# Reading final LSTM states for their transposes straight from the batch-innermost tile, with the score stage unrolled

## The reference, cut to what matters

```python
h = jnp.maximum(_layernorm(x, axis=-1), 0.0)
x = x + _L2_gnn_ref(h, ...)      # LSTMs over windows of 1 to 4 nodes: the final states
h = jnp.maximum(_layernorm(x, axis=-1), 0.0)
x = x + _L3_gnn_ref(h, ...)      # attention over 256 edges
...
# in _L3_gnn_ref
Xq = (H @ W_lin.T).reshape(bt, n, h, dh)
Xv = (H @ W_val.T).reshape(bt, n, h, dh)
Qs = Xq[:, src]
Kt = Xq[:, dst]
e = jnp.einsum('behd,hd->beh', jax.nn.leaky_relu(Qs + Kt, LRELU_SLOPE), a)
```

## Time and profile before

| | us |
|---|---|
| median of 3 runs | 1331.84 (1330.07 to 1332.06) |
| the profiled execution, its own time | 1332.54 |
| its span in the trace | 1330.8 |
| PE busy | 1204.2 (90%) |
| DVE busy | 1047.3 (79%) |
| ACT busy | 944.5 (71%) |
| POOL busy | 381.8 (29%) |
| first instruction of the score stage on ACT, from the span's start | 1015.86 |
| last `q_sums` of the score stage begins | 1174.54 |

### The profile page before, as it was taken

One profiled execution on the slowest core, in us unless ns is written; L12 is line 12 of the kernel. 1 busy time (PEld: TensorE's weight loads), 2 busy tenths in 40 slices (PEclk: granted clock), 3 DMA queues, 4 the chain that ended last, 5 costly groups with the idle time before them and its releaser, 6 DMA issues. The chain is left out here.

```text
span 1330.8 us, 23570 instructions
## 1 busy us (share of the span) xinstructions
PE 1204.2 (90%) x6704; PEld 967.9 (73%) x6704; DVE 1047.3 (79%) x2081; ACT 944.5 (71%) x1745; POOL 381.8 (29%) x770
## 2 busy tenths in 40 slices
PE   3999979979889998999999999999996999936998
PEld 2999876643368886798789878978984777724777
DVE  4777857987778876988798779878874899986775
ACT  2666648857668876877787778767766999814775
POOL 2566750000067420000000000000001566615885
PEclk8999998989979999999999999999997999977999
DMA  7000000000031110000000000003003000000212
GB/s 295 1 0 0 0 0 0 0 0 0 30 113 63 71 41 1 0 1 0 1 0 1 0 1 1 1 0 127 1 0 127 1 1 0 1 0 8 79 71 95
DMA packets 14461, 37.80 MB, mean 28 GB/s; under 512 B 1856, under 2 KB 3904, under 8 KB 13120
## 3 DMA queue, kind: packets, MB, share of 16 engines
q1 hardware_dynamic: 13008, 36.31, 7.1%
q10 hardware_dynamic: 1392, 0.74, 0.2%
HBM read 20.27 MB, written 16.78 MB: 28 GB/s over the span
## 5 line engine op out<-in xcount | busy, mean ns | idle before, releaser
L955 ACT ACTIVATE gates<-bank,lstm_bias 128x512 f32<-128x512 f32 (+1 forms) x504 | 301.8, 637 | 101.8 <-PE bank L944 88.8
L139 ACT ACTIVATE l_h<-X,nmr,rstd 128x128 f32 (+1 forms) x512 | 210.2, 485 | 54.3 <-POOLq L133 32.9
L108 POOL TENSOR_TENSOR l2r_sum<-l2r_st 128x8 f32<-128x8 f32 x16 | 3.4, 210 | 532.8 <-DVE l2r_st L89 532.5
L929 PE MATMUL bank<-lstm_node_hi,Wih_hi 128*128 128x512 f32 (+1 forms) x408 | 149.0, 365 | 0.0
L930 PE MATMUL bank<-lstm_node_hi,Wih_lo 128*128 128x512 f32 (+1 forms) x408 | 148.8, 365 | 0.0
L931 PE MATMUL bank<-lstm_node_lo,Wih_hi 128*128 128x512 f32 (+1 forms) x408 | 148.7, 365 | 0.0
L940 PE MATMUL bank<-lstm_hid_hi,Whh_hi 128*128 128x512 f32 (+1 forms) x288 | 104.2, 362 | 4.7 <-DVE lstm_hid_hi L1011 4.5
L944 PE MATMUL bank<-lstm_hid_lo,Whh_hi 128*128 128x512 f32 (+1 forms) x288 | 106.7, 370 | 0.0
L941 PE MATMUL bank<-lstm_hid_hi,Whh_lo 128*128 128x512 f32 (+1 forms) x288 | 103.3, 359 | 0.0
L960 ACT ACTIVATE gates<-lstm_cell 128x512 f32<-128x512 f32 (+1 forms) x144 | 83.7, 581 | 21.7 <-DVE lstm_cell L998 21.5
L929 PEld LDWEIGHTS bank<-lstm_node_hi,Wih_hi 128*128 128x128 f32 x408 | 76.9, 189 | 11.6 <-ACT gates L955 0.3
(11 more groups left out here) (252 smaller groups left out, 3304.6 us busy)
## 6 DMA issues: line engine op xcount, KB each, us to landing
X<-in_x SPq DMA_DIRECT2D x8, 1024.0 KB, 14.1
x_spill<-X SPq DMA_DIRECT2D x32, 256.0 KB, 2.0
X<-x_spill SPq DMA_DIRECT2D x2, 4096.0 KB, 12.6
out<-X SPq DMA_DIRECT2D x32, 256.0 KB, 2.0
w_raw<-in_WihT SPq DMA_DIRECT2D x1, 1024.0 KB, 5.3
w_raw<-in_WhhT SPq DMA_DIRECT2D x1, 1024.0 KB, 7.5
W<-in_L_W ACTq DMA_DIRECT2D x1, 192.0 KB, 4.8
rows<-in_rows ACTq DMA_DIRECT2D x1, 128.0 KB, 4.3
```

What stands on the lines that cost most here:

```text
L139: last = act.activation(h[:, j, :], k.X[:, bass.ds(b0, TB), :][:, j, :], ACT.Relu, bias=k.nmr[:, bass.ds(b0, TB)][:, j:j + 1], scale=k.rst ...
L929: pe.matmul(out, hi, x_high, start=True, stop=False)
L955: act.activation(gate_of(it, g), k.bank[4 * s + g][:, 0:it.N], ACT.Tanh if g == GATE_G else ACT.Sigmoid, bias=k.lstm_bias[:, it.p - 1, g:g ...
```

## The change

The stage is written out turn by turn with constant addresses (no hardware loops, no register arithmetic, no semaphores counted up by one ahead). `Residual` is no longer used there. ACT's fetch and the two buffers `l2r_o` are gone; PE's transposes take each batch of a tile straight out of `HT`, so the stationary operand is 128 floats a partition with a step of 64 bytes. The waits for the fetch are gone on PE. The order of everything else on each engine is as before, and so is the DMA.

```diff
 def stage_scores(k, ctx, HT, Xv, scores, e):
...
-    res = Residual(k, ctx, "l2r", S, {}, psR)
+    ln = LayerNormTail(k, ctx, "l2r", S)
     tail_in = sem("l3_x_tail")
-    HALF = n_it // 4 - AHEAD // 2
...
+    states = HT[:, :].rearrange("h (g n b) -> h g n b", n=P, b=GROUP)
+    rows = lambda i, s: slice((i * S + s) * TB, (i * S + s + 1) * TB)
+    TAIL = k.B // 2 // (TB * S)
...
         def _(act):
-            def fetched(place, ahead):
-                return in_group(HT, place, ahead).rearrange("h n b -> h b n")
...
+            for i in range(n_it):
                 for s in range(S):
                     act.wait_ge(R["Tp"][s], i + 1)
                     act.activation(hT[s][:, :, :], as_tile(psT[s]), ACT.Copy).then_inc(R["hT"][s], 1)
-                if place:
-                    for s in range(S):
-                        act.wait_ge(res.R_ready[s], i + AHEAD + 1)
-                        res.fetch(act, s, fetched(place, (AHEAD + 1) * S + s))
...
         def _(pe):
+            def turn_over(i, s):
+                if i:
+                    pe.wait_ge(R["updated"][s], i)
+                for j in range(TB):
+                    b = (i * S + s) * TB + j
+                    last = pe.transpose(psR[s][:, j * P:(j + 1) * P], states[:, b // GROUP, :, b % GROUP], k.ident[:, :])
+                last.then_inc(R["R"][s], 1)
+
+            for i in range(AHEAD):
+                for s in range(S):
+                    turn_over(i, s)
+            for i in range(n_it):
                 for s in range(S):
                     pe.wait_ge(R["h"][s], i + 1)
                     for j in range(TB):
                         last = pe.transpose(psT[s][:, j * P:(j + 1) * P], h[s][:, j, :], k.ident[:, :])
                     last.then_inc(R["Tp"][s], 1)
-                    if residual:
-                        pe.wait_ge(res.updated[s], i + AHEAD)
-                        res.turn_over(pe, i + AHEAD, s)
+                    if i + AHEAD < n_it:
+                        turn_over(i + AHEAD, s)
```

More of the change, by code:

```diff
@@ L1189, in _ @@
         def _(pool):
-            def turn(i, place, residual, following):
+            ln.open(pool)
+            for i in range(AHEAD):
+                ln.coefficients(pool, i)
+            for i in range(n_it):
                 for s in range(S):
-                    pool.wait_ge(R["lin"][s], i + 1)
+                    if i:
+                        pool.wait_ge(R["lin"][s], i)
                     pool.wait_ge(R["Xq"][s], i + 1)
@@ L1196, in turn @@
                                        op=ALU.mult).then_inc(R["Qs"][s], 1)
-                if residual:
-                    res.coefficients(pool, i + AHEAD)
-            res.ln.open(pool)
-            for s in range(S):
[L1202 to L1205, removed]
+                if i + AHEAD < n_it:
+                    ln.coefficients(pool, i + AHEAD)
         @block.scalar
         def _(act):
-            def fetched(place, ahead):
-                return in_group(HT, place, ahead).rearrange("h n b -> h b n")
             def normalise(i, s):
-                res.ln.wait(act, s, i)
+                ln.wait(act, s, i)
                 normalise_tile(act, k, h[s], (i * S + s) * TB).then_inc(R["h"][s], 1)
-            def turn(i, place, residual, following):
+            for s in range(S):
+                normalise(0, s)
+            for i in range(n_it):
                 for s in range(S):
@@ L1228, in turn @@
                     act.wait_ge(R["V"][s], i + 1)
-                    act.activation(Xv[:, bass.ds((i * S + s) * TB, TB), :], as_tile(psV[s]), ACT.Copy).then_inc(R["Xv"][s], 1)
-                    if following:
+                    act.activation(Xv[:, rows(i, s), :], as_tile(psV[s]), ACT.Copy).then_inc(R["Xv"][s], 1)
+                    if i + 1 < n_it:
                         normalise(i + 1, s)
[L1233 to L1240, removed]
         @block.tensor
         def _(pe):
-            def turn(i, place, residual, following):
+            def turn_over(i, s):
+                if i:
+                    pe.wait_ge(R["updated"][s], i)
[3 more added lines that the diff above has]
+                last.then_inc(R["R"][s], 1)
+            for i in range(AHEAD):
+                for s in range(S):
+                    turn_over(i, s)
+            for i in range(n_it):
                 for s in range(S):
@@ L1264, in turn, with _, update @@
                         pe.matmul(ps[:, :], e.PT[:, c * P:(c + 1) * P], Xq[s][:, :, :], start=True, stop=True).then_inc(R["G"][s], 1)
-            for s in range(S):
-                pe.sem_inc(R["M"][s], 1)
+        @block.vector
+        def _(dve):
+            def update(i):
+                if i == TAIL:
+                    dve.wait_ge(tail_in, 16)
+                for s in range(S):
+                    xt = X[:, rows(i, s), :]
+                    dve.wait_ge(R["R"][s], i + 1)
+                    dve.tensor_tensor(xt, as_tile(psR[s]), xt, ALU.add).then_inc(R["updated"][s], 1)
+                for s in range(S):
+                    dve.wait_ge(R["updated"][s], i + 1)
+                    ln.stats(dve, X[:, rows(i, s), :], s, i)
             for i in range(AHEAD):
+                update(i)
+            for i in range(n_it):
+                if i + AHEAD < n_it:
+                    update(i + AHEAD)
                 for s in range(S):
                     if i:
[L1271 to L1281, removed]
+                        dve.wait_ge(R["kept"][s], i)
                     for c, ps in enumerate((psQ[s], psV[s])):
@@ L1288, in turn @@
                 for s in range(S):
[L1289 to L1292, removed]
+                    t = i * S + s
+                    dve.wait_ge(R["M"][s], i + 1)
+                    dve.tensor_reduce(scores[:, :, t * HW:(t + 1) * HW], M[s][:, :, :].rearrange("p c (x d) -> p c x d", x=HW),
                                       mybir.AxisListType.X, ALU.add).then_inc(R["kept"][s], 1)
                 for s in range(S):
[L1295 to L1298, removed]
+                    t = i * S + s
+                    dve.wait_ge(R["Qs"][s], i + 1)
+                    dve.tensor_reduce(e.q_sums[:, t * HW:(t + 1) * HW], Qs[s][:, :, :].rearrange("p b (x d) -> p (b x) d", x=HEADS),
                                       mybir.AxisListType.X, ALU.add).then_inc(R["lin"][s], 1)
[L1301 to L1306, removed]
         @block.sync
```

29 lines of the change are left out of this document (8 added, 21 removed).

## The result

| | before | changed |
|---|---|---|
| median of 13 runs each, side by side, us | 1331.45 (1329.94 to 1333.18) | 1328.13 (1326.31 to 1329.51) |
| profiled execution: own time / span, us | 1332.54 / 1330.8 | 1328.55 / 1326.8 |

The ratio is 0.9972, with a 95% interval from 0.9965 to 0.9980. The change makes the kernel faster by 0.28%. I had forecast 8.1 us more with a chance of 0.60 for slower. What came is rival 1 of the prediction, given 0.32 and priced at 1328.6 us. The time lies inside the range; the sign of the forecast is wrong.

A forecast was written before the change was run, and what follows sets the result against it. PE was taken as the bound, DVE just behind. The terms -2.0 (fetches), -1.2 (beginning) and +11.3 (step) gave +8.1 us: 1339.9 us against the median, range 1327.5 to 1345.5.

The forecast's parts named there:

- rival 1: PE's state transposes: the 64-byte step is free for PE, so the kernel gets faster, 1328.6 us; chance 0.32.
- sign of the forecast: Whole kernel: slower, by 8.1 us against the profiled execution; chance 0.60 for slower.
- Fetches removed: Turns 1 to 12: without ACT's fetches each turn is 0.17 us shorter, 2.0 us in all.
- The beginning: Start of the score stage: without the fetch PE starts sooner and statistics come 1.2 us earlier, minus 1.2 us.
- Turn 0: First turn: no gain from the fetches gone, since it waits for the first layernorm and a slow clock.
- Unrolling: Whole stage: register and address instructions vanish, costed at nothing because running matmuls hide them.
- The step: State transposes, turns 1 to 13: strided stationary loads add 0.87 us a turn, 11.3 us in all.
- If the load of PE's weights is held to this, it takes 128 x 1.70 = 218 ns: State transposes: ACT's strided read price of 1.70 ns a float applied to PE's load, against a 109 ns slot.
- A load overlaps the matmul ahead of it, but here both last a slot: State transposes: a load of 218 ns makes the slot 218 ns, 0.109 us more for each transpose.
- low bound of 7.3 us: State transposes: with the 801 ns fetch as contiguous row, 0.55 ns a float excess, 0.070 us on 104 loads.
- ACT is no quicker on contiguous data: Argument against rival 1: ACT, at 0.80 ns a float contiguous against PE's 0.85, still slows to 1.70.
- its first reason: Argument for rival 1: the transposes' 109 ns slot gives PE 0.85 ns a float, slower than ACT's 0.80.

The follow-up runs named there:

- e8: Kernel before, stage written out, ACT's fetch kept, slot 1's fetch moved behind its copy of `Xv`: 1330.31 us, ratio 0.9994 to the kernel before.
- e11: The changed kernel unaltered, run and profiled again beside the kernel before on one chip: 1329.06 us, ratio 0.9978.
- e1: Kernel before with the stage written out, ACT's fetch and contiguous transposes kept: 1332.09 us, ratio 1.0005 to the kernel before.
- e6: Written-out stage with ACT's fetch, its source step varied from 1 to 16 floats by pair of turns; executed once, no total time given.
- e5: Changed kernel, slot 0's transposes narrowed to 32 columns, slot 1's made plain products, step varied by turn; four transposes 0.37 us at step 1, 0.56 at 16.
- e7: Changed kernel, each slot's four state transposes replaced by one 512-wide product with the state tile moving, step varied by pair of turns: 1354.0 us.
- e10: Changed kernel with `hT` stored batch-innermost, so the loads of `Wqv`'s products have a step of 4 floats: 1394.79 us.

## Why the prediction was wrong

- **Fetches removed, -2.0.** Right in mechanism and size. Turns 1 to 13 gave 1.70; the step took back 0.35, so 2.05 came from the fetches. e8 shows the mechanism: `Xq` behind 2 us of copies was the cost.
- **The beginning, -1.2.** Right: -1.26. It is the same 10.33 us in e11.
- **Turn 0, "nothing".** Open. It is about 1 us shorter in three of four traces with the direct read and longer in the fourth, by the clock, which the prediction took for the same before and after. The medians show nothing of it.
- **Unrolling, nothing.** Right, by e1.
- **The step, +11.3.** Wrong: +0.35. The step that failed is "If the load of PE's weights is held to this, it takes 128 x 1.70 = 218 ns". ACT does pay by the step (e6), and the load of a plain product does take 0.21 us (e5). But a transpose's load with the same step takes 0.10 to 0.11 us (e5), which just fits the slot of 0.109, so the slot grew by 0.003 us and not by 0.109.
- **"A load overlaps the matmul ahead of it, but here both last a slot".** This failed with it. I took the pace of 0.109 us for the length of the load. It is that of the 128 moving columns alone; a contiguous transpose load lasts 0.06 us (e5, on 32 partitions), and the step's 0.048 us went into the slack. The low bound of 7.3 us, which puts ACT's excess wholly on top of the slot, failed by this.
- **"ACT is no quicker on contiguous data".** The same mistake in another place: 0.85 ns a float is the pace of the slot; the load reads 128 floats in 0.06 us, under 0.5 ns a float. For the moving operand the comparison was true (e7).
- **The chances.** Rival 1 was described by its condition, "as long as a load stays below 0.109 us", and this is nearly what came: the strided loads are at the edge of it, and cost 0.003 us each. Its name, "free", and its first reason, a pace of 0.85 ns a float, are not exact. By the Trainium skill, TensorE: Matmul & The Clock Gate, section LDWEIGHTS, a load's time goes by its columns alone. The turn agrees, the loads don't: 141 ns became 196, and e5 and e10 show loads of the same 128 columns at 0.06, 0.11, 0.10 and 0.24 us.

A sign was there to read. The record of a transpose's load lasted 141 ns, that of a `PT` load 0.19 us (PEld in the same turn), though both load 128 columns. That the shorter one had slack against an equal slot could have been asked. Nor did I ask whether a transpose's load and a plain float32 product's have one pace.

The sum with the measured terms, turn 0 left out, is -2.05 - 1.26 + 0.35 = -3.0 us, against -3.3 between the medians; the interval of the ratio reaches from -2.7 to -4.7.

## What to carry to other kernels

A pace is the longest of what runs in parallel; it says nothing of how long the hidden partner lasts. Before a dearer access is put into a hidden operation, measure that operation with its cover taken away: e5 did so with a narrow moving operand. A price taken from another engine, or from another kind of product on the same engine, needs the same test. On this kernel a strided stationary operand was nearly free in a transpose and doubled the time of a plain float32 product; a strided moving operand doubled its own. A step of 2 floats was almost free everywhere but in the narrow transposes.

An engine's work may cost by its place in the order, not by its length: 2 us of fetches cost 0.17 us a turn, and moving one of them behind the urgent copy gave that back.

One trace of each kernel can hold a difference that the next trace doesn't have. Turn 0 looked like a microsecond of gain until the same code was profiled again.

## What the runs showed of the hardware that I had not expected

- The load of a transpose's stationary operand is faster than that of a plain float32 product: with 16 floats of step 0.11 us against 0.21, and with 128 contiguous columns 0.06 against 0.10 (e5, the transposes on 32 partitions, the plain products on 128).
- The transposes' loads are at their strided price already at 2 floats (0.59 us for a group of four, as at 4), while plain products and ACT pay little there (0.86 us for 8 loads against 0.81, and 1.25 us against 1.14). Why, no run shows.
- Narrow transposes at 64 and 128 floats were slower still, 0.69 us a group against 0.55 at 32. At 120 floats they took 0.55 again (e5), so it is not the distance as such.
- The clock rose within the same 16 transposes in one execution and not in another (first trace and e11).
